# A macaron layer on eight cores: where one elementwise product of the WKV scan is computed, and how many buffers the LayerNorm statistics load into

## The reference

```python
x = x + 0.5 * ffn(layernorm(x))          # bit-linear feed-forward, C=2048, F=8192
x = x + attn(layernorm(x))               # RWKV time mixing
x = x + 0.5 * ffn(layernorm(x))

def attn(hidden):
    shifted = pad(hidden)[:, :-1]
    xk, xv, xr = (hidden * m + shifted * (1 - m) for m in (mix_k, mix_v, mix_r))
    k, v, r = xk @ Wk.T, xv @ Wv.T, sigmoid(xr @ Wr.T)
    # w = -exp(time_decay), u = time_first; per channel, over the positions:
    #   out = (num + exp(u + k) * v) / (den + exp(u + k))
    #   num = exp(w) * num + exp(k) * v
    #   den = exp(w) * den + exp(k)
    return (r * wkv(k, v)) @ Wo.T
```

## Time and profile before

| | us |
|---|---|
| median of 3 runs | 10253.19 |
| the three runs | 9698.34, 10253.19, 10373.16 |
| the profiled execution | 9698.34 |
| its span (first to last instruction, slowest core) | 9696.8 |
| spans of the eight cores | 9677.0 to 9696.8 |
| mean granted TensorE clock, of full speed | 0.868 to 0.872 |
| the two `ln_stats`, first load to L383 (the first of them) | 4440 to 4496 |
| scan interleaved with the r projection | 5436 to 6032 |

### The profile page before, as it was taken

The page is one execution under the profiler, slowest core; times in us unless marked ns, Lnnn a source line. Parts: engine busy times, 40 slices in busy tenths (PEclk is TensorE's granted clock), DMA queues, the critical chain, the costliest instruction groups (busy, mean ns, idle before and its releaser), DMA issues.

```text
span 9696.8 us, 84809 instructions; the slowest of 8 cores (9677.0 to 9696.8 us)
## 1 busy us (share of the span) xinstructions
PE 6935.1 (72%) x31729; PEld 3201.9 (33%) x31729; DVE 3962.9 (41%) x3923; ACT 1042.2 (11%) x1062; POOL 361.8 (4%) x104
## 2 busy tenths in 40 slices
PE   0021999999992389884359342945999999978888
PEld 0010444444440033331124111422444444433333
DVE  0026555555546523443541665255222222254332
ACT  5541000000000000001001132010000000000000
POOL 0000000000000000000220332000000000000000
PEclk9975999999995589996679676957999999989999
DMA  9975433333326866665423322742111211146666
GB/s 287 310 265 183 155 143 139 139 143 140 145 103 200 255 202 215 215 214 193 144 104 135 111 92 103 218 145 99 71 70 70 79 70 70 70 156 219 210 207 197
DMA packets 390257, 1524.20 MB, mean 157 GB/s; under 512 B 41285, under 2 KB 74454, under 8 KB 289494
## 3 DMA queue, kind: packets, MB, share of 16 engines
q1 hardware_dynamic: 232282, 1183.13, 36.5%
q10 hardware_dynamic: 155136, 327.22, 9.0%
q0 software_dynamic: 2432, 8.42, 0.2%
HBM read 1183.03 MB, written 335.58 MB: 157 GB/s over the span
## 4 chain that ended last, share of the span: by engine, by line
PE 61%; DVE 17%; DMA 13%; ACT 3%; issue 2%; POOL 2%; ACTq 1%; DVEq 0%; SPq 0%; POOLq 0%
PE pb L599 18%; PE pb L606 18%; PE pb L725 14%; PE pb L1066 5%; DMA wbuf<-wgu 4%; DVE tmp L772 3%; PE pb L533 2%; PE pb L1160 2%; DMA wbuf<-wdn 2%; DMA terndn<-tern 2%; DVE bfA L904 1%; DMA gsb<-g1d 1%; DVE tmp L776 1%; DVE bfA L779 1%; ACT wbuf L308 1%
## 5 line engine op out<-in xcount | busy, mean ns | idle before, releaser
L725 PE MATMUL pb<-bfA,tern 128*128 128x512 bf16 x7936 | 1803.2, 390 | 288.7 <-DVE bfA L779 281.7
L599 PE MATMUL pb<-bfA,tern 128*128 128x512 bf16 x8192 | 1856.2, 380 | 9.1 <-DVE tern L566 9.1
L606 PE MATMUL pb<-bfA,tern 128*128 128x512 bf16 x8192 | 1851.6, 379 | 0.0
L725 PEld LDWEIGHTS pb<-bfA,tern 128*128 128x128 bf16 x7936 | 786.3, 100 | 1307.1 <-issue 438.9
L1066 PE MATMUL pb<-bfA,tern 128*128 128x512 bf16 x3072 | 699.0, 392 | 711.6 <-DVE tern L933 456.9
L606 PEld LDWEIGHTS pb<-bfA,tern 128*128 128x128 bf16 x8192 | 801.6, 98 | 966.5
L599 PEld LDWEIGHTS pb<-bfA,tern 128*128 128x128 bf16 x8192 | 802.5, 98 | 867.4 <-issue 18.1
L540 DVE TENSOR_REDUCE macc<-pb 128x4 f32<-128x512 f32 x512 | 354.8, 693 | 1695.9 <-PE pb L533 1651.3
L621 ACT ACTIVATE tmp<-tmp 128x512 f32<-128x512 f32 x512 | 322.2, 629 | 3450.1 <-DVE tmp L616 3450.1
L1066 PEld LDWEIGHTS pb<-bfA,tern 128*128 128x128 bf16 x3072 | 307.4, 100 | 1104.3 <-issue 764.9
L744 DVE TENSOR_TENSOR tmp<-pb,bcst 128x512 f32<-128x512 f32 x128 | 88.5, 692 | 1226.1 <-PE pb L725 1213.2
(11 more groups left out here) (131 smaller groups left out, 3684.3 us busy)
## 6 DMA issues: line engine op xcount, KB each, us to landing
tern<-terndn SPq DMA_DIRECT2D x496, 512.0 KB, 4.4
wbuf<-wgu SPq DMA_DIRECT2D x64, 2048.0 KB, 11.4
wbuf<-wdn SPq DMA_DIRECT2D x128, 1024.0 KB, 7.0
wbuf<-wgu SPq DMA_DIRECT2D x128, 1024.0 KB, 10.1
g1d<-gsb ACTq DMA_DIRECT2D x512, 256.0 KB, 2.7
gsb<-g1d SPq DMA_DIRECT2D x128, 1024.0 KB, 5.4
terngu<-tern ACTq DMA_DIRECT2D x128, 512.0 KB, 9.0
tern<-terngu SPq DMA_DIRECT2D x128, 512.0 KB, 4.4
```

Source lines behind the costliest of these rows:

```text
L599: p.op("tensor", lambda e, g=g, t=t, tt=ta, ba=ba: e.matmul(out=pb[ba][:], lhsT=TT(tt)[:, g * 128:(g + 1) * 128], rhs=AR(g)[:, t * 512:(t ...
L606: p.op("tensor", lambda e, g=g, t=t, tt=tb_, bb=bb: e.matmul(out=pb[bb][:], lhsT=TT(tt)[:, g * 128:(g + 1) * 128], rhs=AR(g)[:, t * 512:(t ...
L725: bb=bk: e.matmul(out=pb[bb + l][:], lhsT=TT(sl)[:, ko * 512 + l * 128: ko * 512 + (l + 1) * 128], rhs=AR512(og), start=(og == 0), stop=(o ...
```

## The change

Two independent edits.

1. `ln_stats` uses two float32 buffers, both in `gsb`: the load of chunk g waits for chunk g-2. Nothing else of the loop changes.
2. In the scan, `st_bv` = b*v is no longer a POOL product of b and v. ACT computes it as exp(u) * `st_av`, one activation with a per-partition scale, emitted right behind the decay (L983). The count `ew_ac`, for which DVE's scans wait, is now read after this activation. The addition num + `st_bv` and its one-column copy are emitted ahead of the addition den + b. POOL's next a*v additionally waits for ACT's new activation, which reads `st_av`, and the loads wait for POOL's L973 of block dg-2 where they waited for L1012.

```diff
@@ ln_stats
-            ISL = (GS(0), GS(1), WS(0), WS(1))
-            ISEM = ("LG0", "LG1", "LW0", "LW1")
             for g in range(NG):
                 sl = g % 2
-                isl = g % 4
-                sem = ISEM[isl]
-                if g >= 4:
-                    p.wait("sync", "DV", cdv[g - 4])
-                    p.wait("sync", "AC", cac[g - 4])
-                p.dma("sync", sem, lambda e, g=g, isl=isl: e.dma_start(
-                    out=ISL[isl], in_=src(g)))
+                sem = f"LG{sl}"
+                if g >= 2:
+                    p.wait("sync", "DV", cdv[g - 2])
+                    p.wait("sync", "AC", cac[g - 2])
+                p.dma("sync", sem, lambda e, g=g, sl=sl: e.dma_start(out=GS(sl),
+                                                                     in_=src(g)))
@@ proj_era, emit_scan_loads
-                p.wait("sync", "PL", scan_pl_bv.get(dg - 2, mix_pl0))
+                p.wait("sync", "PL", scan_pl_av.get(dg - 2, mix_pl0))
...
                 p.wait("gpsimd", "DV", scan_nacc_dv.get(dg - 1, 0))
+                p.wait("gpsimd", "AC", scan_bv_ac.get(dg - 1, 0))
@@ proj_era, emit_scan
                     out=t_ew, in_=tmp[:, 0:1024], func=AF.Identity, scale=0.0,
                     bias=cols[:, CEW + dg:CEW + dg + 1]))
+                p.wait("scalar", "PL", scan_pl_av[dg])
+                p.wait("scalar", "DV", scan_num_dv.get(dg - 1, 0))
+                p.op("scalar", lambda e, dg=dg: e.activation(
+                    out=st_bv, in_=st_av, func=AF.Identity,
+                    scale=cols[:, 112 + dg:112 + dg + 1]))
+                bv_ac = p.cnt["AC"]
+                scan_bv_ac[dg] = bv_ac
                 ew_ac = p.cnt["AC"]
                 p.wait("vector", "AC", ew_ac)
...
                 scan_ac[dg] = p.cnt["AC"]
-                p.wait("gpsimd", "AC", scan_ac[dg])
-                p.wait("gpsimd", "DV", scan_num_dv.get(dg - 1, 0))
-                p.op("gpsimd", lambda e, st_b=st_b, st_v=st_v: e.tensor_tensor(
-                    out=st_bv, in0=st_b, in1=st_v, op=ALU.mult))
-                scan_pl_bv[dg] = p.cnt["PL"]
+                p.wait("vector", "AC", bv_ac)
+                p.op("vector", lambda e: e.tensor_tensor(
+                    out=t_num2[:, 1:2048], in0=t_nacc2[:, 0:2047],
+                    in1=st_bv[:, 1:2048], op=ALU.add))
+                p.op("vector", lambda e: e.tensor_copy(
+                    out=t_num2[:, 0:1], in_=st_bv[:, 0:1]))
+                scan_num_dv[dg] = p.cnt["DV"]
                 p.wait("vector", "AC", scan_ac[dg])
                 p.op("vector", lambda e, st_b=st_b: e.tensor_tensor(
                     out=t_den2[:, 1:2048], in0=t_dacc2[:, 0:2047],
...
                 den_dv = p.cnt["DV"]
-                p.wait("vector", "PL", scan_pl_bv[dg])
-                p.op("vector", lambda e: e.tensor_tensor(
-                    out=t_num2[:, 1:2048], in0=t_nacc2[:, 0:2047],
-                    in1=st_bv[:, 1:2048], op=ALU.add))
-                p.op("vector", lambda e: e.tensor_copy(
-                    out=t_num2[:, 0:1], in_=st_bv[:, 0:1]))
-                scan_num_dv[dg] = p.cnt["DV"]
```

More of the change, by code:

```diff
@@ L360, in ln_stats @@
                 p.wait("vector", "PE", p.cnt["PE"] - 8 if g >= 1 else 0)
-                p.op("vector", lambda e, sl=sl, isl=isl: e.tensor_copy(
-                    out=TT(sl), in_=ISL[isl]))
+                p.op("vector", lambda e, sl=sl: e.tensor_copy(out=TT(sl), in_=GS(sl)))
                 cdv[g] = p.cnt["DV"]
@@ L365, in ln_stats @@
                 p.wait("scalar", "PE", p.cnt["PE"] - 8 if g >= 1 else 0)
-                p.op("scalar", lambda e, sl=sl, isl=isl: e.activation(
-                    out=TT(2 + sl), in_=ISL[isl], func=AF.Square))
+                p.op("scalar", lambda e, sl=sl: e.activation(out=TT(2 + sl), in_=GS(sl),
+                                                             func=AF.Square))
                 cac[g] = p.cnt["AC"]
@@ L951, in proj_era @@
             scan_ac = {}
+            scan_bv_ac = {}
             scan_pl_bv = {}
```

## The result

The changed kernel takes 0.4% longer than the kernel before: ratio 1.004, 95% interval 1.0025 to 1.0055, which on 9698 us is +39 us (+24 to +53). The medians over all runs are 10218.1 (12 runs, 9734.4 to 10680.7) and 10178.1 us (13 runs, 9698.3 to 10403.4).

A forecast was written before the change was run, and what follows sets the result against it. PE, 61% of the chain, was taken to carry the time, with both edits in stages other engines set. Scan +13 and statistics +18 gave +31 us on 9698.3, so 9729 us; range 9650 to 10410.

The forecast's parts named there:

- the case of 0.65: Whole kernel: scan +13 us and statistics +18 us give +31 us, 9729 us; chance 0.65.
- the base that the sum stands on: Whole kernel: the profiled execution's 9698.3 us, lowest of the runs shown (9698, 10253, 10373), to which +31 us is added.
- the length of a statistics pass: `ln_stats` with two slots: 18.6 + 8L, with landing L = 5.8 us, gives 65.0 us a pass, +9.2.
- Removed from the scan's chain, 5.37 us: Scan block, end of L1000 to start of L1036: old path 16.19 us, new path 10.82, so 5.37 us saved.
- Added, 2.09: Scan block: ACT's new product, 2.00 us plus about 0.09 for the step, delays the scans by 2.09 us.
- Moved, 4.1: Scan block: POOL's next L973 starts after the num scan and makes L1000 wait, +4.1 us; bounds 0 and 4.33.
- the first rival: Scan: POOL finds room beside the scans, or gets in only during DVE's reciprocal wait; 9668 us, chance 0.26.
- Sum of the scan, +13: Scan: 15 blocks at +0.8 us, +12, and the last at +1 give +13 us; bounds +17 and -48.
- The statistics, +18: `ln_stats`: two passes, each 65.0 us and +9.2, cost +18 us together; bounds +6 and +54.
- L + 2.1: `ln_stats`, one slot's cycle: landing L (5.8 us), 0.1 to wake ACT, 1.91 square, 0.1 to the next issue.
- The rival of long landing: `ln_stats`: two loads take as long as four, L = 10.0 us, both passes +86, total 9797 us; chance 0.06.

## Why the prediction was right or wrong

The forecast was +31 us on the profiled execution, 9729, within 2% of before and by the case of 0.65. Measured is +39 (+24 to +53), best run 9734.4. The case was the right one, and so was the sign of the sum. Two steps failed, and both are sizes. The first is the base that the sum stands on, 9698.3, the lowest of three runs: the medians are 10218 after and 10178 before, so that as a time 9729 is 5% too low, and beside the median before it even reads as a gain, where the measured change is a loss of 0.4%. The second is the length of a statistics pass, 65.0 forecast and 67 to 69 measured, told below. The range held the median only because its upper end was carried to the slowest run shown; that end was reasoned from the spread of the kernel before and not from the change, and that it held is luck.

Step by step:

- *Removed from the scan's chain, 5.37 us.* The block without the stall measures 33.28 with the activation in the chain, 36.57 + 2.09 - 33.28 = 5.38. Right. (The reading ahead of it is off: 5622.73 - 5621.50 is 1.23 us and not 1.1; no sum uses it.)
- *Added, 2.09.* The wait ahead of the scans rose from 4.75 to 6.84. Right, and moving the activation off it gave 33.28 - 31.18 = 2.10 back.
- *Moved, 4.1, the term that rested on a guess.* Measured 6.34 - 2.35 = 3.99. The kernels with POOL's product at three places bear out the reason: the stall sits with whichever DVE instruction of two SBUF inputs comes behind that product, scan or addition, and vanishes where DVE is idle. Here the rule of the Trainium skill (SBUF — State Buffer, section "Who interferes with whom") held for an instruction that it doesn't name. That POOL gets in between two DVE instructions 0.11 us apart (L1002 ends at 5615.21, L1005 starts at 5615.32 and waits) also rules out the other half of the first rival.
- *Sum of the scan, +13.* Measured +10.5 between the first and the last L1042, where the forecast has 14 blocks at +0.8 and the last at +1: +12. The block is +0.7 and not +0.8, the 0.1 of the stall.
- *The statistics, +18.* Measured +24. The term that was mis-sized is the length of a pass with two buffers, 65.0 forecast and 66.3 on core 0, 68.0 and 67.2 on average over the four cores. It was not the cycle: L + 2.1 = 7.9 forecast, and from the square of chunk 1 to that of chunk 15 the seven cycles take 7.64 each on core 0 (median landing 5.4 in the first pass), 7.94 and 7.77 on average. It was the two ends. "Chunk 15 is issued 0.4 after the start plus 7 cycles" lets the first load of the second slot land as fast as the later ones. It was issued beside that of chunk 0 and took 8.1 us, so the square of chunk 1 starts 8.59 us after the first issue (4441.46 - 4432.87; 8.2 and 8.6 on average) and not 0.4 + 5.8 + 0.1 = 6.3. And the first read of the sums follows the start of the last square by 4499.21 - 4494.97 = 4.24 us and not by the 4496.08 - 4492.69 = 3.39 of the earlier trace rows. With these, 8.59 + 7 x 7.64 + 4.24 = 66.3.
- *The rival of long landing* is out: 5.4, not 10.0.

Why that tail is 0.85 us longer: the earlier trace rows shows an uncommon one. In that pass the last eight column sums ran at a granted clock of 1.00 (2.4 GHz), 0.38 us each:

```profile
4494.74 0.38 PE L372 MATMUL pb<-tern,constsb_s 128*1 128x512 bf16 x1 [0.63 <-ACT tern L366]
```

In the changed kernel the last eight ran at 0.50 (1.2 GHz), 0.58 to 0.63 us each (the chain above has one at 4497.03, 0.59). Before, PE's clock was 0.50 too from 4446 to 4486, and rose only behind that. Of the sixteen passes before, two on each core, four have a tail of 3.4 us and twelve one of 4.2; all eight passes of the changed kernel on this die have 4.2.

What stays open is the difference of 4 us between the 35 found in the two stages and the 39 of the ratio; the interval of the ratio is wider than that.

## What to carry to other kernels

When a product is taken from one engine's queue to another, ask what the freed engine does next: here the multiply that was removed from POOL let POOL's other multiply start earlier, right beside a scan, and it took back 4.0 of the 5.4 us saved; a wait that sends it into DVE's idle time turned +0.7 us a block into -3.3. And ask for which count the next consumer waits: an activation put between a producer and the reading of its count joins the chain (2.1 us), though nobody downstream needs it yet. For a load loop, compare a slot's cycle (landing plus hold) over the number of slots with the time of a transfer alone: with 7.5 us a cycle and 3.5 us a megabyte (55.8 us for 16 with four slots, both ends included), two slots fall short (3.75), three suffice (2.5), and the fourth brought 1 us in 56.

## What the runs showed of the hardware

A POOL TENSOR_TENSOR of 128x2048 float32 and a DVE TENSOR_TENSOR_SCAN of 128x1024 exclude each other as POOL and a two-input addition do: POOL keeps its 4.30 us, and the scan behind it takes 6.34 us in place of 2.35, 3.99 more. POOL gets its turn in a gap of 0.11 us between two DVE instructions, while a one-column copy runs through at 0.15 us. What I hadn't expected is how exactly the stall moves with POOL's start: 6.34 on a scan, 6.14 on an addition, none in a 5.51 us idle stretch that is longer than the product (4.51).
